# Splitting six PSUM banks four and two, in place of three and three, between two kinds of attention scores

## The reference, cut to what matters

```python
scores = jnp.einsum('bhqd,bhkd->bhqk', q, k) / jnp.sqrt(jnp.float32(DK))
scores = jnp.where(mask == 0, -jnp.inf, scores)
weights = jax.nn.softmax(scores, axis=-1)
weights = jnp.nan_to_num(weights, nan=0.0)
attn = jnp.einsum('bhqk,bhkd->bhqd', weights, v)
x = x + _L0_xattn_ref(_layernorm(x), ctx, ctx, mask, ...)   # masked: stage xa0
x = x + _L0_ffn_ref(_layernorm(x), ...)                     # stages sa0 (attention), me0 (experts)
x = x + _L1_xattn_ref(_layernorm(x), ctx, ctx, ...)         # stage xa1
x = x + _L1_ffn_ref(_layernorm(x), ...)                     # stage me1
```

## Time and profile before

| | |
|---|---|
| runs | 1202.46, 1204.26, 1214.95 us; median 1204.26 |
| profiled execution | 1207.72 us, span of its instructions 1206.0 us |
| mean granted TensorE clock | 0.931 |
| TensorE, VectorE, ScalarE, GpSimd busy | 89%, 65%, 50%, 16% of the span |

### The profile page before, as it was taken

The page is one execution under the profiler, slowest core; times in us unless marked ns, Lnnn a source line. Parts: engine busy times, 40 slices in busy tenths (PEclk is TensorE's granted clock), DMA queues, the critical chain, the costliest instruction groups (busy, mean ns, idle before and its releaser), DMA issues. The chain is left out here.

```text
span 1206.0 us, 17909 instructions
## 1 busy us (share of the span) xinstructions
PE 1076.1 (89%) x5834; PEld 546.5 (45%) x5834; DVE 784.5 (65%) x1960; ACT 608.5 (50%) x1293; POOL 187.0 (16%) x250
## 2 busy tenths in 40 slices
PE   7989999999898999999859999996989999998380
PEld 4533333333463334444546667664633444445260
DVE  4778887875678798995642222214688989957632
ACT  2236666666432677777413233331327877774250
POOL 2100000000200021231411222211100010102255
PEclk9979999999997799999859999998989999999695
DMA  8954523320087354542740220103983433202064
GB/s 299 321 153 106 135 65 91 65 59 2 1 269 255 92 130 107 132 107 63 277 175 21 102 97 27 34 5 107 298 261 92 100 68 89 67 15 70 23 178 140
DMA packets 72922, 141.74 MB, mean 118 GB/s; under 512 B 9148, under 2 KB 26176, under 8 KB 71424
## 3 DMA queue, kind: packets, MB, share of 16 engines
q1 hardware_dynamic: 68752, 130.36, 36.8%
q0 software_dynamic: 4080, 10.23, 3.1%
HBM read 86.30 MB, written 52.17 MB: 115 GB/s over the span
## 5 line engine op out<-in xcount | busy, mean ns | idle before, releaser
L932 ACT ACTIVATE r<-ps 128x512 f32<-128x512 f32 x768 | 417.5, 597 | 194.9 <-PE ps L1033 193.9
L404 DVE TENSOR_REDUCE m<-ps 128x1 f32<-128x512 f32 x512 | 322.0, 684 | 38.7 <-PE ps L1002 38.5
L1002 PE MATMUL ps<-stacks 48*128 48x512 f32 x720 | 291.4, 481 | 4.5 <-DVE r L481 3.0
L1033 PE MATMUL ps<-stacks 50*128 50x512 f32 x768 | 286.3, 465 | 8.3 <-DMA stacks<-mT 4.7
L1042 PE MATMUL ps<-r 128*32 128x512 f32 x1536 | 210.6, 621 | 1.5 <-ACT r L932 1.5
L1033 PEld LDWEIGHTS ps<-stacks 50*128 50x128 f32 x768 | 122.1, 192 | 184.6 <-ACT r L932 124.2
L400 DVE CUSTOM_DVE_ANT_0 r<-ps,r 128x512 bf16<-128x512 f32 x256 | 166.0, 688 | 43.7 <-PE ps L1002 42.0
L1002 PEld LDWEIGHTS ps<-stacks 48*128 48x128 f32 x720 | 119.2, 194 | 26.1 <-DVE m L404 14.8
L890 POOL COPY r<-r 128x256 f32<-128x256 f32 x48 | 19.3, 406 | 545.2 <-PE ps L1042 521.7
L607 ACT ACTIVATE r<-ps,cols 128x512 fp32r<-128x512 f32 x48 | 33.0, 688 | 115.4 <-PE ps L668 113.2
L668 PE MATMUL ps<-r,w 128*128 128x512 f32 x192 | 90.5, 609 | 0.5 <-issue 0.5
(11 more groups left out here) (150 smaller groups left out, 1088.2 us busy)
## 6 DMA issues: line engine op xcount, KB each, us to landing
stacks<-q_parts SPq DMA_DIRECT2D x96, 192.0 KB, 3.6
stacks<-k_parts SPq DMA_DIRECT2D x96, 192.0 KB, 4.4
k_parts<-r SPq DMA_DIRECT2D x24, 512.0 KB, 3.5
q_parts<-r SPq DMA_DIRECT2D x24, 512.0 KB, 4.4
r<-in_w SPq DMA_DIRECT2D x16, 512.0 KB, 3.7
r<-in_w SPq DMA_DIRECT2D x8, 1024.0 KB, 11.3
k_parts<-r SPq DMA_DIRECT2D x24, 256.0 KB, 3.9
q_parts<-r SPq DMA_DIRECT2D x24, 256.0 KB, 4.3
```

The lines of the kernel that those rows point to most:

```text
L404: ins = dve.tensor_reduce(out, mem.ps[:, bank, :], AX.X, ALU.max)
L932: act.activation(mem.probs[:, u // HG, u % HG, :], ps[:, ST + unit_of(b, g, u) % DEEP, :], ACT.Exp, scale=SCALE).then_inc(a.p_exp.sem, 1)
L1002: pe.matmul(ps[:, led_bank(n), :], stack_of(mem.qst[g], h, ROWS)[:, t * P:(t + 1) * P], stack_of(mem.kst[g], h, ROWS), start=True, stop=Tr ...
L1033: pe.matmul(ps[:, ST + N % DEEP, :], stack_of(mem.kst[g], h, KROWS)[:, kt * P:(kt + 1) * P], stack_of(mem.qst[g], h, KROWS), start=not a.m ...
```

## The change

In the masked stage banks 0 to 3 hold transposed scores and 4 and 5 ordinary ones. `DEEP` is replaced by `a.deep_t` and `a.deep_s`, which are 4 and 2 there and 3 and 3 in the two other attention stages. A pair of transposed scores now waits for the exponential of unit N + 1 - 4, an ordinary score for the maximum two before it. The lead-in's mask transposes stay in bank 2, so a wait on the copy out of it is put before unit 2. The transpose of the first maxima stays after the fourth leading score.

```diff
+        self.deep_t = 4 if masked else 3
+        self.SB, self.deep_s = ST + self.deep_t, OB - self.deep_t
...
-DEEP = 3
-ST, SB = 0, DEEP
-OB = 2 * DEEP
+ST, OB = 0, 6
...
-def led_bank(n):
+def led_bank(a, n):
 
-    return SB + n % DEEP
+    return a.SB + n % a.deep_s
...
     def bank_free(N):
 
-        if N >= DEEP:
-            pe.wait_ge(a.p_exp.sem, a.p_exp.at(0, N - DEEP + 1))
+        if N >= a.deep_t:
+            pe.wait_ge(a.p_exp.sem, a.p_exp.at(0, N - a.deep_t + 1))
 
     def masks(b, g, u):
 
         N, kt = unit_of(b, g, u), u // HG
         bank_free(N + 1)
+        if N == 2:
+            pe.wait_ge(a.mbT_ready.sem, a.mbT_ready.at(b, MASK_ROUNDS))
...
-        for bank, mask, turned in ((ST + N % DEEP, mem.mbT, 0), (ST + (N + 1) % DEEP, mem.mbX, 1)):
+        for bank, mask, turned in ((ST + N % a.deep_t, mem.mbT, 0), (ST + (N + 1) % a.deep_t, mem.mbX, 1)):
...
-                    scores(s, v, N, (0, N - DEEP + LEAD))
+                    scores(s, v, N, (0, N - a.deep_s + LEAD))
...
     for v in range(LEAD - UNITS):
-        if a.masked and v == DEEP + 1:
+        if a.masked and v == 4:
             pe.wait_ge(a.mbT_ready.sem, a.mbT_ready.at(0, 1))
-            turn_mask(0, 1, ST + DEEP - 1)
-        if v < DEEP:
-            bank = led_bank(UNITS - LEAD + v)
+            turn_mask(0, 1, ST + 2)
+        if v < a.deep_s:
+            bank = led_bank(a, UNITS - LEAD + v)
             pe.wait_ge(a.r1.sem, a.r1.at(B - 1, bank - QK_BANK + 1))
-        scores(1, v, UNITS - LEAD + v, (1, v - DEEP) if v >= DEEP else None)
-        if v == DEEP:
+        scores(1, v, UNITS - LEAD + v, (1, v - a.deep_s) if v >= a.deep_s else None)
+        if v == 3:
             maxima(0)
```

More of the change, by code:

```diff
@@ L931, in exps @@
             act.wait_ge(a.pv.sem, a.pv.at(G - 1, u // HG + 1))
-        act.activation(mem.probs[:, u // HG, u % HG, :], ps[:, ST + unit_of(b, g, u) % DEEP, :], ACT.Exp,
+        act.activation(mem.probs[:, u // HG, u % HG, :], ps[:, ST + unit_of(b, g, u) % a.deep_t, :], ACT.Exp,
                        scale=SCALE).then_inc(a.p_exp.sem, 1)
@@ L972, in attend_scalar @@
     if a.masked:
-        mask_copy(0, 0, ST + DEEP - 1)
+        mask_copy(0, 0, ST + 2)
     maxima(0)
     if a.masked:
-        mask_copy(0, 1, ST + DEEP - 1)
+        mask_copy(0, 1, ST + 2)
     body(0, True, False)
@@ L1001, in scores @@
             pe.wait_ge(a.s_max.sem, a.s_max.at(used[0], used[1] + 1))
-        pe.matmul(ps[:, led_bank(n), :], stack_of(mem.qst[g], h, ROWS)[:, t * P:(t + 1) * P],
+        pe.matmul(ps[:, led_bank(a, n), :], stack_of(mem.qst[g], h, ROWS)[:, t * P:(t + 1) * P],
                   stack_of(mem.kst[g], h, ROWS), start=True, stop=True).then_inc(a.s_ps.sem, 1)
     def bank_free(N):
-        if N >= DEEP:
-            pe.wait_ge(a.p_exp.sem, a.p_exp.at(0, N - DEEP + 1))
+        if N >= a.deep_t:
+            pe.wait_ge(a.p_exp.sem, a.p_exp.at(0, N - a.deep_t + 1))
     def masks(b, g, u):
@@ L1032, in transposed_scores @@
             masks(b, g, u)
-        pe.matmul(ps[:, ST + N % DEEP, :], stack_of(mem.kst[g], h, KROWS)[:, kt * P:(kt + 1) * P],
+        pe.matmul(ps[:, ST + N % a.deep_t, :], stack_of(mem.kst[g], h, KROWS)[:, kt * P:(kt + 1) * P],
                   stack_of(mem.qst[g], h, KROWS), start=not a.masked, stop=True).then_inc(a.st_ps.sem, 1)
@@ L1136, in attend_tensor @@
         pe.wait_ge(a.mbS_ready.sem, a.mbS_ready.at(0, T))
[L1137 removed]
+        turn_mask(0, 0, ST + 2)
     for v in range(LEAD - UNITS):
[L1139 removed]
+        if a.masked and v == 4:
             pe.wait_ge(a.mbT_ready.sem, a.mbT_ready.at(0, 1))
[L1141 to L1143 removed]
+            turn_mask(0, 1, ST + 2)
+        if v < a.deep_s:
+            bank = led_bank(a, UNITS - LEAD + v)
             pe.wait_ge(a.r1.sem, a.r1.at(B - 1, bank - QK_BANK + 1))
[L1145 to L1146 removed]
+        scores(1, v, UNITS - LEAD + v, (1, v - a.deep_s) if v >= a.deep_s else None)
+        if v == 3:
             maxima(0)
@@ L1219, in body @@
                         mask_for_maxima(dve, a, b + 1, v)
-                    maximum(dve, a, led_group, v, led_bank(unit_of(b, g, u)))
+                    maximum(dve, a, led_group, v, led_bank(a, unit_of(b, g, u)))
                     if v == UNITS - 1:
@@ L1232, in attend_vector @@
     for v in range(LEAD - UNITS):
-        maximum(dve, a, 1, v, led_bank(UNITS - LEAD + v))
+        maximum(dve, a, 1, v, led_bank(a, UNITS - LEAD + v))
     body(0, True, False)
```

## The result

| | before | after |
|---|---|---|
| median of 15 runs | 1206.54 us (1201.12 to 1214.95) | 1218.38 us (1215.46 to 1220.91) |
| profiled execution's span | 1206.0 us | 1216.1 us |
| mean granted clock in it | 0.931 | 0.933 |

The ratio is 1.0096 with a 95% interval of 1.0079 to 1.0113: 1% slower, 11.8 us by the medians and 10.1 us by the two spans. The forecast was 9.1 us more, and a time of 1213.4 us.

A forecast was written before the change was run, and what follows sets the result against it. TensorE was busiest (89%), but VectorE's maxima ended level with it in the masked stage, so two banks could not shorten the cycle. Losses of 11.0 us less gains of 1.9 gave +9.1 on 1204.3: 1213.4 us, range 1204 to 1221.

The forecast's parts named there:

- (a): Plain four-unit cycles of the masked stage: second pair's scores held for maxima, 0.16 us longer in 16 cycles, 2.6 us.
- (b): After a group's quotients, second pair following directly: score held by the late maximum, 0.30 us in 5 cycles, 1.5 us.
- (c): After quotients where projections or transposes fill TensorE: no wait given back, 0.51 us in 8 cycles, 4.1 us.
- (d): Four transposes between pairs, third pair of g = 1 in three batches: late load only, 0.09 us each, 0.3 us.
- (e): Three groups where VectorE also makes the next batch's mask, two with residual: score held, 0.73 us each, 2.2 us.
- two further places: Where a residual meets a maximum in a batch's last group: a loss of 0.15 us each, 0.3 us.
- (f): Waits saved at the stage's half-clock start, 0.8 us, and behind 289.2 us after the maxima, 1.1 us: together 1.9 us.
- faster rival: Masked stage: ScalarE waits go and nothing replaces them, 1193 us, or half of it, 1199 us; chance 0.07 for both.
- (g): Twelve scores ahead of the stage through two banks: 2.2 us later, covered by 2.42 us of TensorE idling; costs nothing.
- clock rival: Masked stage: long holds drop TensorE's clock in three groups, 4.75 us each, one fall 1218 us, three 1227; chance 0.13.

The follow-up runs named there:

- e1: Changed kernel with three instead of four banks for transposed scores, two for maxima-scores, one unused; ratio 1.0095 to the kernel before, long part (units 16 to 228) 209.18 us.
- e8: Changed kernel with each masked-stage maximum over 256 of 512 keys; long part (units 16 to 228) 191.39 us, one execution of 1205.89 us.
- e3: Kernel before, three and three banks, with each masked-stage maximum over 256 of 512 keys; ratio 0.9967 to the kernel before, long part 198.06 us.
- e9: Kernel before, three and three banks, with some products with V cut into halves of 256 queries; ratio 0.9965 to the kernel before, long part 194.40 us.
- e12: e9 with the transpose of the maxima after unit 5 instead of 9 in seven groups; ratio 0.9941 to the kernel before, long part 193.11 us.
- e5: Changed kernel with VectorE's quotients behind the group's last maximum instead of ahead of it; ratio 1.0059 to the kernel before, long part 206.07 us.
- e6: Changed kernel with VectorE's four next-mask conversions before every second maximum instead of four in a row; ratio 1.0078 to the kernel before, long part 208.26 us.
- e10: Kernel before, three and three banks, with a second pair's masks put in one at a time; ratio 1.0002 to the kernel before, long part 198.34 us.
- e4: Kernel before, three and three banks, with all masked-stage products with V cut into halves of 256 queries; ratio 1.0142 to the kernel before, long part 220.26 us.

## Why the prediction was right

**What bounds the cycle.** The reading of the earlier trace rows, that maximum and score lie 10 ns apart and that two banks therefore can't shorten the cycle, holds in every part: e1 shows that the bank taken is all of the loss in the long part, e8 and e3 that it is VectorE's time.

**The terms.** Pair by pair in the two traces: (a) was put at 0.16 us, and the cycle is 3.70 instead of 3.54. (b) 0.30, measured 0.28 (masks 265.86 to 269.67, 3.81 us, against 3.53). (c) 0.51, measured 0.52: in most of the eight 0.10 for a hold at the last pair of the group ahead and 0.42 after the first pair. (d) 0.09, measured 0.10. (e) 0.73, measured 0.78, 0.68 and 0.68. The two further places 0.15, measured 0.18. The losses up to unit 228 were put at 11.0 us. The stretch grew by 10.6, which with the 0.9 us gained at half clock is 11.5. The 0.5 us between them lies in the first group, whose last five pairs, partly at half clock, took 0.8 us longer where two plain cycles make 0.3. In the long part alone the terms come to 10.6 us, and 10.7 were measured. So the agreement isn't luck: it holds term by term.

**The gains (f)** were put at 0.8 and 1.1 us and came out at 0.9 (the first three pairs take 1.73, 1.80 and 1.73 us instead of 2.05 each) and 1.4 (22.44 to 21.03 us). The second is larger as a wait's row shows only the time with the array idle: the two waits that make 1.1 us in the list were 0.5 and 0.75 us from start to start, and a third, of 0.16, wasn't in the list at all. For the same reason the waits behind the transpose, which the faster rival takes at 0.19 us, were 0.26 from start to start (a pair of 1.53 us became 1.27).

**The lead-in (g)** was put at nothing under a cover of 2.42 us. In the changed kernel that idle time is 0.55 us, as the timeline shows:

```profile
72.57 1.40 PE L1002 MATMUL ps<-stacks 48*128 48x512 f32 x2 [0.18 <-DVE m L402]
74.52 0.64 PE L1024 MATMUL ps<-r,identb 64*64 64x512 bf16 x4 [0.55 <-DMA stacks<-mT]
```

The later transpose and the slower round trip took 1.9 us of the cover, and the transfer's landing still ends it. The stage starts 0.6 us later than in the trace of before. Of this, 0.4 us is not the wait that (g) speaks of: SyncE's queue issues the transfer behind others that were 0.38 us later already, 69.49 after 65.73 where it was 69.09 after 65.35.

```profile
65.73 1.47 SPq L351 DMA_DIRECT2D stacks<-q_parts  x2
...
69.49 1.40 SPq L806 DMA_DIRECT2D stacks<-mT  x2
```

The kernels with three and three banks start at 72.47 to 75.11 and those with four and two at 72.92 to 74.53, so what else of it is the change's stays open.

**Rivals.** The clock did not fall: 1.00 throughout the long part, in spite of its 57 held scores, the longest by 0.74 us. TensorE: Matmul & The Clock Gate of the Trainium skill (a second failure mode), which tells of clock swings from cycling through PSUM banks, isn't borne out by this trace.

One thing in the prediction's reading of the clock was wrong. It says that TensorE ran at 0.50 from 74.0 us on after it had been idle for 2.42 us. The table by stretch of the kernel before shows that the clock was at 0.50 from 66.4 us on, five microseconds ahead of that idle time, after a stretch in which TensorE was busy for 5.20 of 6.40 us:

```profile
60.00:66.40 6.40, 5.20 (x28) 2.59 (x27) 6.24 (x19) 2.15 (x4) 0.00 (x0) 1.00 0.65 255
66.40:71.48 5.08, 4.90 (x13) 2.06 (x10) 4.80 (x17) 1.12 (x2) 0.00 (x0) 0.50 1.05 237
71.48:73.90 2.42, 0.00 (x0) 0.00 (x0) 0.99 (x4) 0.00 (x0) 0.00 (x0) 0.50 1.05 246
```

So the idle time at 71.48 did not bring the clock down. In the changed kernel it is only 0.55 us long, and the half clock is there all the same, from 67.2 to 84.3 us. The price of the clock rival, 9.5/2 us a fall, counts only the part of such a period that lies in the stage; by the whole 17.1 us from 66.4 to 83.5 it would have been some 8.5 us. Nothing in the forecast's sum rests on this.

Of the faster rival only the two ends came about. It would have needed a faster VectorE. With one, in e8, the long part is 7.1 us shorter than before, most of the way to what that rival counts on.

**The size.** The spans differ by 10.1 us, the medians by 11.8. The runs of one kernel differ with the mean granted clock: the changed kernel took 1215.46 us at 0.935 and 1220.71 and 1220.91 at 0.929. The difference between 10.1 and 11.8 is within that. The time itself came out 5.0 us above the 1213.4 of the forecast: 2.3 of them because the median of the kernel before moved from 1204.26 us in three runs to 1206.54 in fifteen, 2.7 because the change costs 11.8 by the medians instead of 9.1. With 0.96% the change lies just inside the 1% line.

## What to carry to other kernels

Before a bank is moved from one buffer to another, compare for the one that loses it when its consumer ends and when its producer comes back: if these are level, the second buffer is the next bound and the move only swaps waits. A wait that comes from an uneven rhythm of the producer is better met by evening out the rhythm (e9, e12) than by depth, and with shallow buffers the order of the consumer's side work begins to count (e5, e6). Read waits from start to start: rows of overlapping products hide them, and a held product can cost its late weight load on top.

## What the runs showed of the hardware

- A held score that is the last of its pair costs 0.09 us beyond its wait: the next instruction follows its load after 0.42 to 0.43 us instead of 0.33. One that is the first of its pair is followed by the next transposed score after the usual 0.34 us (271.34 to 271.68 in the changed kernel). About the same 0.09 us came in e10, where nothing was held but mask products stood between the two scores.
- Two mask products of 64 x 64 cost as much as four: 0.33 us to the next start in e10, 0.34 in the earlier trace rows. Eight products with V of 256 columns take 0.57 us (255.02 to 255.59), eight of 512 take 1.00.
- VectorE's maximum with the mask takes 0.69 us for 512 columns and 0.42 for 256. If the time grows evenly with the columns, some 0.15 us of it don't depend on them, an estimate from these two.
- In the profiled execution of e4 TensorE, once at half clock at the stage's start, stayed there until about 123 us, where the kernels before and after were back at full clock at about 84 us and the others between 82 and 89. The table by stretch of e4:

```profile
70.00:80.00 10.00, 6.49 (x26) 2.48 (x27) 5.78 (x21) 2.17 (x4) 0.00 (x0) 0.50 0.87 176
80.00:125.00 45.00, 44.17 (x264) 14.09 (x266) 22.36 (x70) 18.39 (x35) 0.70 (x2) 0.52 0.27 75
```

Its execution took 1242 us at a mean clock of 0.918, the other five 1223 to 1234. The mean granted clock of e4's fastest run was 0.938, so the long half clock was not in all of them; what decided it, I can't say. The length of e4's long part in the table, 220.26 us, has this half clock in it.
